# First feed-forward network's weights: product and low half moved from GpSimd to VectorE, two layer norms moved with them, one ScalarE wait later, and other lengths in the planner's list

## The chip, the cores and the metric

The kernel runs on one core of one Trainium2 chip. The metric is device time in microseconds (us), as the median of several executions. The engines are named TensorE (PE), VectorE (DVE), ScalarE (ACT), GpSimd (POOL) and SyncE (SP) in the text and by the short names in the profile.

## What is computed

Two transformer layers on x of shape (4, 512, 512), each with two sublayers and a layer norm after each sum:

```python
x = layernorm(x + L0_attn(x))    # causal attention, 32 query heads, 8 key heads, head size 16, rotary
x = layernorm(x + L0_ffn(x))     # 512 -> 1376 -> 512, SiLU gate; weights packed as 4-bit numbers
x = layernorm(x + L1_attn(x))    # a "hydra" state-space mixer, two passes
x = layernorm(x + L1_ffn(x))     # 512 -> 1792 -> 512, SiLU gate; weights as int32 with scale and zero
```

The weights of the first feed-forward network (FFN) are `w = q*s - (z+1)*s`, where q is one of eight 4-bit numbers in an int32, s a float16 scale and z a 4-bit zero. Those of the second are `(w - z)*s`.

## The kernel before

**Tiling.** The 2048 tokens are 16 tiles of 128. Attention runs in 352 units; a unit is a group of heads of one query tile (scores in PSUM, `nmax`, `exp`, transposes `ptr`, a high half `pth` and a low half `ptl` in float16, then `pv`). Matrices are held as a float16 high half and a float16 low half, so each product of an FFN takes three matmuls.

**Order of the work.** The class `Stream` (from line 169) is a planner that runs on the host while the kernel is built. It lists every step with its engine, an assumed length in ns, what it waits for and a rank. `place()` (line 407) runs the list by events: each engine takes, of its ready steps, the one with the lowest rank. The result is one fixed order for each engine, and each engine executes its own order strictly, waiting on semaphores where the real lengths differ from the assumed ones. So a wait of one step holds back everything listed behind it on that engine. The assumed lengths are no instructions: they only decide the order. For SP a step holds the engine for `SP_ISSUE` (1300 ns for all kinds) and ends after its listed length. `START_AT` says when each engine's stream begins.

**First FFN's weights.** They come in 27 chunks (`CH0`, line 146): 16 of 128x688 for gate and up, 11 of 128x512 for down (the last of 96 rows). Chunk c has rank 2c-2, so the planner ties two attention units to each chunk. A chunk runs: three loads by SP (`sp_w0`, lines 702 to 711: packed numbers to `pk`, zeros to `zb`, scales to the low half's place); VectorE takes the 4 bits out (L1166) and forms q minus z (L1169); GpSimd multiplies by the scale (`pool_dequant`, L839, to `wv`); ScalarE rounds the high half (L1043); GpSimd subtracts to get the low half (`pool_dequant_lo`, L846). `wv`, `pk`, `zb` and `nib` have two buffers. The first gate and up matmul of the first FFN (L1538) waits for the low half of the last chunk (`w0_lo`, NC0), since all of w0 must be there.

**Second FFN's weights.** 84 chunks of 128x256, after the last chunk of the first: three loads by SP (L720 to L722), three operations on GpSimd (L851, L853, L855: `w1_q`), the high half on ScalarE (L1048, which also waits for the stores of the chunk before), the low half on GpSimd (L859), two stores to DRAM (L727, L728). Two buffers. They are loaded back as whole matrices only when the first FFN is done with its gate and up matmuls.

**Norms.** `bn1` and `bn2` gather mean and variance on VectorE (L1133 to L1136); GpSimd forms 1/sqrt (L872) and normalises (L874), for all 16 tiles and both norms of the first layer. The norms of the second layer form 1/sqrt on GpSimd and normalise on VectorE (L1381, L1408).

**Start.** VectorE unpacks the zeros of the first FFN (L1438, L1442), SP stores them to DRAM (L817). ScalarE issues six small loads, then waits for all three stores, then starts its stream with the copy `xT` of the first tile (L979), for which the first projections (L1498) wait. The buffers of the zeros lie where `xh`, `xl`, `attn`, `aT` and `wo` are used later; VectorE and GpSimd have waits of their own on the stores.

Of the kernel before, what the change touches and what calls it, by code (L numbers as in the profile page):

```python
# [79 lines left out]
RING = 8  # L80
# [92 lines left out]
class Stream:  # L173
# [46 lines left out]
    def weights0(self):  # L220
        A = self.add
        for c, (k, g, c0, n) in enumerate(CH0):
            r = CH0_AT[c]
            A("SP", "w0", c, 3000, [("deq", c - 2)] if c >= 2 else [], r - 6)
            A("DVE", "deq", c, 1500 if n == HW else 1200, [("w0", c)], r)
            A("POOL", "deq_w", c, 1600 if n == HW else 1230, [("deq", c), ("w0_lo", c - 2) if c >= 2 else None], r)
            A("ACT", "w0_hi", c, 780 if n == HW else 600, [("deq_w", c)], r)
            A("POOL", "w0_lo", c, 1600 if n == HW else 1230, [("w0_hi", c)], r)

    def weights1(self):  # L230
        A = self.add
        for c in range(NC1):
            r = CH1_AT[c]
            A("SP", "w1c", c, 3000, [("w1_lo", c - 2) if c >= 2 else ("w0_lo", NC0 - 1)], r - 6)
            A("POOL", "w1_q", c, 1950, [("w1c", c)], r)
            A("ACT", "w1_hi", c, 420, [("w1_q", c), ("w1s", c - 1) if c else None], r)
            A("POOL", "w1_lo", c, 720, [("w1_hi", c)], r)
            A("SP", "w1s", c, 2500, [("w1_lo", c)], r)
# [22 lines left out]
    def attention(self, u):  # L261
        A = self.add
        t, i, w, h, g = UNITS[u]
        c = w * g
        need = [("e" + kind, t) for kind in STAGE]
        A("PE", "score", u, 0.42 * c + 55 * g, need + [("exp", u - 2) if u >= 2 else None], u)
        A("DVE", "nmax", u, 150 + 1.07 * c, [("score", u), ("exp", u - 4) if u >= 4 else None], u - 1)
        A("ACT", "exp", u, 200 * g + 0.75 * c, [("nmax", u), ("ptr", u - 2) if u >= 2 else None], u - 1)
        A("PE", "ptr", u, 110 * c // P, [("exp", u), ("ptl", u - 2) if u >= 2 else None], u + 2.1)
        A("ACT", "pth", u, 170 + 0.84 * c, [("ptr", u), ("pv", u - 3) if u >= 3 else None], u)  # L270
        A("DVE", "ptl", u, 150 + 1.07 * c, [("pth", u)], u)
        q = group_of(u)
        new = h % OG == 0
        A("PE", "pv", u, 52 * (i + 1) * g, [("ptl", u), ("out", q - 1) if new and q else None], u + 4.2)
        if ends_group(u):
            A("DVE", "out", q, 620, [("pv", u), ("attn", q - 2) if q >= 2 else None], u)
            A("POOL", "attn", q, 500, [("out", q), ("atr", t - 2) if q % NOG == 0 and t >= 2 else None], u)

    def way_out(self, t):
        A, r = self.add, END[t] + 5  # L280
        A("PE", "atr", t, 440, [("attn", NOG * t + NOG - 1)], r, takes=1)
        A("ACT", "ate", t, 610, [("atr", t), ("wo", t - 1, WO_PIECES - 1) if t else None], r, frees=("atr", t))
        e = self.pieces("wo", t, WO_PIECES, 860, [("ate", t)], r)
        A("DVE", "x1_sum", t, 690, [e], r, frees=("wo", t))
        A("DVE", "bn1", t, 1100, [("x1_sum", t), ("x1", t - 2) if t >= 2 else None], r)
        A("POOL", "x1", t, 1500, [("bn1", t)], r - 4)

    def ffn0(self, h):
# [17 lines left out]
        for x in (0, 1):  # L306
# [6 lines left out]
            A("POOL", "x2_sum", t, 1400, [("y16", t), ("x1", t)], soon - 4)  # L313
            A("DVE", "bn2", t, 1100, [("x2_sum", t), ("x2", t - 2) if t >= 2 else None], soon)
            A("POOL", "x2", t, 1500, [("bn2", t)], soon - 4)
# [100 lines left out]
    def place(self):  # L416
# [40 lines left out]
        while done < len(self.steps):  # L457
# [17 lines left out]
            at[e] = t + (SP_ISSUE if e == "SP" else ns + GAP)  # L475
# [22 lines left out]
SLACK, GAP, SP_ISSUE = 150, 0, 1300  # L498
START_AT = {"PE": 5100, "ACT": 6400, "DVE": 12600, "POOL": 5100, "SP": 15000}
# [10 lines left out]
def build(nc, A):  # L510
# [12 lines left out]
    with ctx:  # L523
# [308 lines left out]
        def pool_dequant(pool, c):  # L832
            k, g, c0, n = CH0[c]
            r = rows0(k, g)
            hi, lo = (w0[k][p][0:r, g, c0:c0 + n] for p in (0, 1))
            pool.wait_ge(sem("deq_z"), c + 1)
            if c >= 2:
                pool.wait_ge(sem("w0_lo"), c - 1)
            pool.tensor_tensor(wv[0:r, c % 2, 0:n], hi, lo, ALU.mult).then_inc(sem("deq_w"), 1)  # L839

        def pool_dequant_lo(pool, c):
            k, g, c0, n = CH0[c]
            r = rows0(k, g)
            hi, lo = (w0[k][p][0:r, g, c0:c0 + n] for p in (0, 1))
            pool.wait_ge(sem("w0_hi"), c + 1)
            pool.tensor_tensor(lo, wv[0:r, c % 2, 0:n], hi, ALU.subtract).then_inc(sem("w0_lo"), 1)  # L846

# [13 lines left out]
        def pool_job(pool, kind, key):  # L861
# [5 lines left out]
            if kind in ("x1", "x2"):  # L867
                n, v, r, m = ("1", ve, rstd, mv) if kind == "x1" else ("2", veb, rstdb, mvb)
                o = key % 2
                x = xr[:, key % RING, :]  # L870
                pool.wait_ge(sem(f"ve{n}"), key + 1)
                pool.tensor_tensor(r[:, o:o + 1], v[:, o:o + 1], neghalf[:, 0:1], ALU.pow).then_inc(sem(f"rstd{n}"), 1)  # L872
                pool.wait_ge(sem(f"rstd{n}"), key + 1)
                pool.tensor_scalar(x, x, m[:, o, 0:1], r[:, o:o + 1], ALU.subtract, ALU.mult).then_inc(sem(kind), 1)  # L874
# [31 lines left out]
        def pool_stream(pool):  # L906
            for name in STREAM.order["POOL"]:
                kind, key = name[0], name[1]
                if kind in ("x1", "x2", "x2_sum", "attn", "f0_lo", "qk", "q_lo", "k_lo"):
                    pool_job(pool, kind, key)  # L910
                if kind == "deq_w":
                    pool_dequant(pool, key)
                if kind == "w0_lo":
                    pool_dequant_lo(pool, key)
# [108 lines left out]
        def act_attention(act, kind, u):  # L1023
# [6 lines left out]
            if kind == "exp":  # L1030
                act.wait_ge(sem("nmax"), u + 1)
# [86 lines left out]
        def _(act):  # L1118
# [7 lines left out]
            for k in "gud":  # L1126
                act.wait_ge(sem(f"st_zs_{k}"), 16)
# [34 lines left out]
        def dve_dequant(dve, c):  # L1162
# [7 lines left out]
                                     in1=zb[0:r, c % 2, 0:n], op0=ALU.mult, op1=ALU.subtract).then_inc(sem("deq_z"), 1)  # L1170

# [14 lines left out]
        def dve_job(dve, own, kind, key):  # L1186
# [41 lines left out]
            if kind == "bn1":  # L1228
                dve.wait_ge(sem("x1_sum"), t + 1)
                if t >= 2:  # L1230
                    dve.wait_ge(sem("x1"), t - 1)
                layer_norm_1(dve, own, x, st6, mv[:, o, :], ve[:, o:o + 1], sem("ve1"))
            if kind == "fxl":
# [4 lines left out]
            if kind == "bn2":  # L1238
                dve.wait_ge(sem("x2_sum"), t + 1)
                if t >= 2:  # L1240
                    dve.wait_ge(sem("x2"), t - 1)
                layer_norm_1(dve, own, x, st6b, mvb[:, o, :], veb[:, o:o + 1], sem("ve2"))
# [167 lines left out]
        def dve_stream(dve, own):  # L1410
            for name in STREAM.order["DVE"]:
# [3 lines left out]
                if kind in ("qk_c", "qk_s", "v", "etq1", "etk1", "x1_sum", "bn1", "fxl", "bn2"):  # L1415
# [3 lines left out]
                if kind == "deq":  # L1419
                    dve_dequant(dve, key)  # L1420
                if kind in ("consts_a", "consts_b", "consts_c"):
# [365 lines left out]
```

## Time and profile before

| | |
|---|---|
| median of 3 runs | 1624.26 us (1624.23 to 1624.38) |
| profiled execution's own time | 1626.21 us |
| its span | 1624.0 us |
| PE busy | 1454.7 us (90%) |
| DVE busy | 1081.7 us (67%) |
| ACT busy | 802.8 us (49%) |
| POOL busy | 773.4 us (48%) |
| mean granted TensorE clock | 0.957 of full |

The span is the profiled execution from its first to its last instruction. The busy share of an engine is a mean over stages with different limits; the stages are the first 184 us (first attention units beside the unpacking of the first FFN's weights), then up to about 880 us attention beside the first FFN and the second FFN's weights, then the hydra stages and the second FFN.

### The profile page before, as it was taken

To read this page: it belongs to the slowest core of one execution; us is meant where nothing else is said; L and a number is where in the kernel's file an instruction comes from. 1 tells how busy PE (TensorE), PEld (TensorE's weight loads), DVE (VectorE), ACT (ScalarE), POOL (GpSimd) and SP (SyncE) were. 2 spreads that over 40 slices of the span, in tenths; PEclk is the share of its full clock that TensorE was granted. 3 is DMA by queue.
4 is the path that set the end of the run, shared out by engine and by line. 5 is a ranking of instruction groups with operands and counts; after the bars stand their busy time and mean duration, and the time that the engine had idled before them with its cause. 6 is when DMAs were issued, how large, how long until landed. Compare 5 with 4: busy or idle time off the path is not lost.

```text
span 1624.0 us, 33859 instructions
## 1 busy us (share of the span) xinstructions
PE 1454.7 (90%) x12464; PEld 1081.9 (67%) x12464; DVE 1081.7 (67%) x2353; ACT 802.8 (49%) x1723; POOL 773.4 (48%) x918
## 2 busy tenths in 40 slices
PE   4767899978899889999999989569999999999998
PEld 2555676766676678686886857337666776857865
DVE  4898776755666667675877876757779679772121
ACT  2566666755656667675766843223333433412211
POOL 3776666566566666666222136424343343332211
PEclk9878799999999999999999999869999999999999
DMA  5433233233433232332002000450100000100000
GB/s 188 128 104 95 67 80 91 67 75 94 105 79 81 68 92 62 104 88 88 9 2 72 28 30 14 175 187 2 34 7 14 27 14 1 40 7 8 14 14 14
DMA packets 94221, 100.34 MB, mean 62 GB/s; under 512 B 11565, under 2 KB 76672, under 8 KB 94056
## 3 DMA queue, kind: packets, MB, share of 16 engines
q1 hardware_dynamic: 92818, 98.10, 21.2%
q8 instruction: 100, 1.64, 0.4%
q14 instruction: 65, 0.53, 0.1%
q10 hardware_dynamic: 1238, 0.07, 0.1%
HBM read 78.70 MB, written 19.43 MB: 60 GB/s over the span
## 4 chain that ended last, share of the span: by engine, by line
PE 40%; DVE 22%; POOL 13%; DMA 11%; issue 6%; SPq 5%; ACT 3%; DVEq 0%; ACTq 0%; POOLq 0%
PE ps L1703 10%; PE ps L1538 5%; PE ps L1601 4%; DMA vs<-in_s1g 4%; DMA vs<-in_s1u 3%; PE ps L1723 3%; PE ps L1553 3%; PE ps L1525 2%; PE ps L1591 2%; DVE xraw L1324 2%; DMA vs<-in_s1d 2%; POOL xr L874 2%; POOL vl L859 2%; PE ps L1651 2%; POOL vq L851 2%
## 5 line engine op out<-in xcount | busy, mean ns | idle before, releaser
L1159 DVE TENSOR_REDUCE nmax<-ps 128x1 f32<-128x384 f32 (+3 forms) x352 | 218.9, 634 | 83.1 <-PE ps L1594 79.9
L1035 ACT ACTIVATE Pe<-ps,nmax 128x256 f32<-128x256 f32 (+3 forms) x512 | 247.0, 535 | 31.3 <-DVE nmax L1159 30.2
L1029 ACT ACTIVATE pth<-ps 128x512 f16<-128x512 f32 (+1 forms) x352 | 196.7, 561 | 130.7 <-PE ps L1601 127.2
L1154 DVE TENSOR_TENSOR ptl<-ps,pth 128x512 f16<-128x512 f32 (+1 forms) x352 | 217.4, 632 | 32.9 <-ACT pth L1029 30.8
L1601 PE MATMUL ps<-identf,Pe 128*128 128x128 f32 x1280 | 208.8, 283 | 10.2 <-DVE ptl L1154 10.0
L1591 PE MATMUL ps<-kT,qT 128*128 128x256 f16 (+3 forms) x512 | 142.2, 311 | 35.1 <-ACT Pe L1035 34.5
L1601 PEld LDWEIGHTS ps<-identf,Pe 128*128 128x128 f32 x1280 | 144.6, 147 | 42.0 <-issue 20.8
L941 POOL TENSOR_TENSOR int1l<-prod,int1h 128x256 f16<-128x256 f32 x112 | 86.4, 776 | 175.6 <-ACT int1h L1115 175.6
L1703 PE MATMUL ps<-x3h,w1gh 128*128 128x256 f16 x448 | 123.3, 275 | 4.9 <-DVE prod L1394 3.8
L1703 PE MATMUL ps<-x3h,w1uh 128*128 128x256 f16 x448 | 123.4, 275 | 0.0
L1703 PE MATMUL ps<-x3l,w1gh 128*128 128x256 f16 x448 | 123.4, 275 | 0.0
L1703 PE MATMUL ps<-x3h,w1gl 128*128 128x256 f16 x448 | 123.3, 275 | 0.0
L1703 PE MATMUL ps<-x3l,w1uh 128*128 128x256 f16 x448 | 123.3, 275 | 0.0
L1703 PE MATMUL ps<-x3h,w1ul 128*128 128x256 f16 x448 | 123.2, 275 | 0.0
L851 POOL TENSOR_TENSOR vq<-vq,vz 128x256 int32<-128x256 int32 x84 | 61.1, 727 | 115.4 <-DMA vs<-in_s1g 47.2
L1109 ACT ACTIVATE sg<-ps 128x256 f32<-128x256 f32 x112 | 42.2, 380 | 147.1 <-PE ps L1703 146.6
L1394 DVE SCALAR_TENSOR_TENSOR prod<-ps,sg 128x256 f32<-128x256 f32 x112 | 46.9, 424 | 99.5 <-ACT sg L1109 94.6
L1614 PE MATMUL ps<-V,pth 128*128 128x34 f16 x1280 | 92.5, 180 | 17.0 <-DVE ptl L1154 15.7
L1614 PEld LDWEIGHTS ps<-V,pth 128*128 128x128 f16 x1280 | 86.6, 98 | 30.2 <-DVE ptl L1154 20.2
L866 POOL TENSOR_TENSOR int0l<-prod,int0h 128x256 f16<-128x256 f32 (+1 forms) x88 | 60.4, 687 | 90.1 <-ACT int0h L1016 89.9
L1594 PE MATMUL ps<-mask,identb 128*128 128x128 bf16 x512 | 102.4, 226 | 0.0
L1115 ACT ACTIVATE int1h<-prod 128x256 f16<-128x256 f32 x112 | 46.0, 417 | 109.2 <-DVE prod L1394 109.2
(236 smaller groups left out, 4067.1 us busy)
## 6 DMA issues: line engine op xcount, KB each, us to landing
xr<-in_x SPq DMA_DIRECT2D x16, 256.0 KB, 4.8
x_dram<-xr SPq DMA_DIRECT2D x16, 256.0 KB, 2.0
x2a<-x_dram SPq DMA_DIRECT2D x4, 1024.0 KB, 4.8
x<-x_dram SPq DMA_DIRECT2D x4, 1024.0 KB, 5.1
out<-x SPq DMA_DIRECT2D x16, 256.0 KB, 2.0
vq<-in_q1g SPq DMA_DIRECT2D x28, 128.0 KB, 2.2
vz<-in_z1g SPq DMA_DIRECT2D x28, 128.0 KB, 3.9
vs<-in_s1g SPq DMA_DIRECT2D x28, 128.0 KB, 4.5
```

The costliest lines, as they stand in the source:

```text
L851: pool.tensor_tensor(q.bitcast(I32), q.bitcast(I32), vz[:, c % 2, :], ALU.subtract).then_inc(sem("w1_i"), 1)
L941: pool.tensor_tensor(int1[1][:, j, :], prod1[:, key % 2, :], int1[0][:, j, :], ALU.subtract).then_inc(sem("f1_lo"), 1)
L1029: act.activation(pth[:, u % 3, 0:g * w], ps[:, 2 + u % 2, 0:g * w], ACT.Copy).then_inc(sem("pth"), 1)
L1035: ins = act.activation(Pe[:, u % 2, x * w:(x + 1) * w], ps[:, u % 2, x * w:(x + 1) * w], ACT.Exp, bias=nmax[:, u % 4, x:x + 1])
L1154: dve.tensor_tensor(ptl[:, u % 3, 0:g * w], ps[:, 2 + u % 2, 0:g * w], pth[:, u % 3, 0:g * w], ALU.subtract).then_inc(sem("ptl"), 1)
L1159: dve.tensor_reduce(nmax[:, u % 4, 0:g], ps[:, u % 2, 0:g * w].rearrange("p (g w) -> p g w", g=g), AX, ALU.max, negate=True).then_inc(sem( ...
L1538: ins = pe.matmul(ps[0:r, bank, cols], w0[m][pw][:, k, c0:c0 + r], px[:, k, :], start=(k == 0 and at == 0), stop=(k == KD - 1 and at == 2))
L1591: pe.matmul(ps[:, u % 2, x * w:(x + 1) * w], qT[:, h // 2, i * P:(i + 1) * P], kT[:, 2 * (h // NREP) + h % 2, first:first + w], start=True ...
L1594: ins = pe.matmul(ps[:, u % 2, at:at + P], identb[:, :], mask[:, :], start=False, stop=True)
L1601: ins = pe.transpose(ps[:, 2 + u % 2, c:c + P], Pe[:, u % 2, c:c + P], identf[:, :])
L1614: ins = pe.matmul(dst, src[:, u % 3, c:c + P], V[:, b % 2, token_tile(b, i, p), h // NREP, :], start=(part == 0 and p == 0), stop=(part == ...
L1703: ins = pe.matmul(ps[:, bank, piece * H2:piece * H2 + H2], w1[m][pw][:, k, j * P:(j + 1) * P], px[:, k, h * H2:h * H2 + H2], start=(at == ...
```

## The change

1. **Unpacking.** L839 and L846 leave GpSimd; the same two `tensor_tensor` operations stand on VectorE as `dve_product` and `dve_low_half`, with the same waits. A chunk is then VectorE four times and ScalarE once.
2. **ScalarE's wait** for the three stores of the zeros moves from ahead of its stream to ahead of the first `exp`.
3. **Norms 1 and 2.** GpSimd keeps 1/sqrt (`rstd1`, `rstd2`), VectorE normalises (`x1`, `x2`). The waits of `bn1` and `bn2` on the norm two tiles earlier go, as both are now in VectorE's own order.
4. **The planner's lengths.** Loads of the first FFN's chunks 6500 instead of 3000 ns, of the second's 5700 instead of 3000, its stores 3600 instead of 2500, `attn` 430 instead of 500, `x2_sum` 1200 instead of 1400; SP held 850 to 4500 ns by kind instead of 1300; VectorE's stream starts at 13100 instead of 12600, SP's at 17500 instead of 15000.

```diff
-            A("SP", "w0", c, 3000, [("deq", c - 2)] if c >= 2 else [], r - 6)
-            A("DVE", "deq", c, 1500 if n == HW else 1200, [("w0", c)], r)
-            A("POOL", "deq_w", c, 1600 if n == HW else 1230, [("deq", c), ("w0_lo", c - 2) if c >= 2 else None], r)
+            A("SP", "w0", c, 6500, [("deq", c - 2)] if c >= 2 else [], r - 6)
+            A("DVE", "deq", c, 1500 if n == HW else 1150, [("w0", c)], r)
+            A("DVE", "deq_w", c, 900 if n == HW else 690, [("deq", c), ("w0_lo", c - 2) if c >= 2 else None], r)
             A("ACT", "w0_hi", c, 780 if n == HW else 600, [("deq_w", c)], r)
-            A("POOL", "w0_lo", c, 1600 if n == HW else 1230, [("w0_hi", c)], r)
+            A("DVE", "w0_lo", c, 900 if n == HW else 690, [("w0_hi", c)], r)
...
-            A("SP", "w1c", c, 3000, [("w1_lo", c - 2) if c >= 2 else ("w0_lo", NC0 - 1)], r - 6)
+            A("SP", "w1c", c, 5700, [("w1_lo", c - 2) if c >= 2 else ("w0_lo", NC0 - 1)], r - 6)
...
-            A("SP", "w1s", c, 2500, [("w1_lo", c)], r)
+            A("SP", "w1s", c, 3600, [("w1_lo", c)], r)
...
-            A("POOL", "attn", q, 500, [("out", q), ("atr", t - 2) if q % NOG == 0 and t >= 2 else None], u)
+            A("POOL", "attn", q, 430, [("out", q), ("atr", t - 2) if q % NOG == 0 and t >= 2 else None], u)
...
-        A("POOL", "x1", t, 1500, [("bn1", t)], r - 4)
+        A("POOL", "rstd1", t, 600, [("bn1", t)], r - 4)
+        A("DVE", "x1", t, 570, [("rstd1", t)], r - 4)
...
-            A("POOL", "x2_sum", t, 1400, [("y16", t), ("x1", t)], soon - 4)
+            A("POOL", "x2_sum", t, 1200, [("y16", t), ("x1", t)], soon - 4)
             A("DVE", "bn2", t, 1100, [("x2_sum", t), ("x2", t - 2) if t >= 2 else None], soon)
-            A("POOL", "x2", t, 1500, [("bn2", t)], soon - 4)
+            A("POOL", "rstd2", t, 600, [("bn2", t)], soon - 4)
+            A("DVE", "x2", t, 570, [("rstd2", t)], soon)
...
-            at[e] = t + (SP_ISSUE if e == "SP" else ns + GAP)
+            at[e] = t + (SP_ISSUE.get(name[0], 450) if e == "SP" else ns + GAP)
...
-SLACK, GAP, SP_ISSUE = 150, 0, 1300
-START_AT = {"PE": 5100, "ACT": 6400, "DVE": 12600, "POOL": 5100, "SP": 15000}
+SLACK, GAP = 150, 0
+SP_ISSUE = {"w0": 1900, "w1c": 1300, "w1s": 850, "weights_a": 4500, "weights_b": 1700, "w1_load": 1300}
+START_AT = {"PE": 5100, "ACT": 6400, "DVE": 13100, "POOL": 5100, "SP": 17500}
...
-            if kind in ("x1", "x2"):
-                n, v, r, m = ("1", ve, rstd, mv) if kind == "x1" else ("2", veb, rstdb, mvb)
+            if kind in ("rstd1", "rstd2"):
+                v, r = (ve, rstd) if kind == "rstd1" else (veb, rstdb)
                 o = key % 2
-                x = xr[:, key % RING, :]
-                pool.wait_ge(sem(f"ve{n}"), key + 1)
-                pool.tensor_tensor(r[:, o:o + 1], v[:, o:o + 1], neghalf[:, 0:1], ALU.pow).then_inc(sem(f"rstd{n}"), 1)
-                pool.wait_ge(sem(f"rstd{n}"), key + 1)
-                pool.tensor_scalar(x, x, m[:, o, 0:1], r[:, o:o + 1], ALU.subtract, ALU.mult).then_inc(sem(kind), 1)
+                pool.wait_ge(sem("ve1" if kind == "rstd1" else "ve2"), key + 1)
+                pool.tensor_tensor(r[:, o:o + 1], v[:, o:o + 1], neghalf[:, 0:1], ALU.pow).then_inc(sem(kind), 1)
...
             if kind == "exp":
+                if u == 0:
+                    for k in "gud":
+                        act.wait_ge(sem(f"st_zs_{k}"), 16)
                 act.wait_ge(sem("nmax"), u + 1)
...
             act.wait_ge(sem("consts"), 1)
-            for k in "gud":
-                act.wait_ge(sem(f"st_zs_{k}"), 16)
             act_stream(act)
...
+        def dve_product(dve, c):
+            k, g, c0, n = CH0[c]
+            r = rows0(k, g)
+            hi, lo = (w0[k][p][0:r, g, c0:c0 + n] for p in (0, 1))
+            dve.wait_ge(sem("deq_z"), c + 1)
+            if c >= 2:
+                dve.wait_ge(sem("w0_lo"), c - 1)
+            dve.tensor_tensor(wv[0:r, c % 2, 0:n], hi, lo, ALU.mult).then_inc(sem("deq_w"), 1)
+
+        def dve_low_half(dve, c):
+            k, g, c0, n = CH0[c]
+            r = rows0(k, g)
+            hi, lo = (w0[k][p][0:r, g, c0:c0 + n] for p in (0, 1))
+            dve.wait_ge(sem("w0_hi"), c + 1)
+            dve.tensor_tensor(lo, wv[0:r, c % 2, 0:n], hi, ALU.subtract).then_inc(sem("w0_lo"), 1)
...
             if kind == "bn1":
                 dve.wait_ge(sem("x1_sum"), t + 1)
-                if t >= 2:
-                    dve.wait_ge(sem("x1"), t - 1)
                 layer_norm_1(dve, own, x, st6, mv[:, o, :], ve[:, o:o + 1], sem("ve1"))
+            if kind in ("x1", "x2"):
+                m, r = (mv, rstd) if kind == "x1" else (mvb, rstdb)
+                dve.wait_ge(sem("rstd1" if kind == "x1" else "rstd2"), t + 1)
+                dve.tensor_scalar(x, x, m[:, o, 0:1], r[:, o:o + 1], ALU.subtract, ALU.mult).then_inc(sem(kind), 1)
```

## Rows read from the trace of the kernel before

**Rows 1.** Stretches: busy PE, PEld, DVE, ACT, POOL (instructions), clock, DMA share, GB/s.

```profile
0.00:40.00 40.00, 19.06 (x76) 11.59 (x76) 16.60 (x45) 8.38 (x12) 15.40 (x26) 0.95 0.61 191
40.00:184.00 144.00, 104.13 (x908) 76.20 (x909) 128.78 (x204) 90.45 (x191) 100.34 (x80) 0.80 0.36 99
184.00:880.00 696.00, 649.78 (x6484) 499.13 (x6483) 462.42 (x944) 444.07 (x981) 406.30 (x569) 0.99 0.29 74
880.00:1100.00 220.00, 179.01 (x1391) 130.13 (x1389) 159.95 (x379) 99.77 (x186) 81.12 (x67) 0.88 0.24 85
```

**Rows 2.** What TensorE waited for, 184 to 880 us: total us, times, longest.

```profile
PE ps L1591 <- ACT Pe L1035: 22.3, 20, 3.1
PE ps L1484 <- POOL attn L888: 8.2, 6, 2.4
```

**Rows 3.** The same of ScalarE.

```profile
ACT vh L1048 <- POOL vq L855: 47.8, 22, 4.8
ACT vh L1048 <- DMA w_ul<-vl: 18.0, 8, 4.6
```

**Rows 4.** The same of GpSimd.

```profile
POOL vq L851 <- DMA vs<-in_s1g: 47.2, 21, 4.4
...
POOL vq L851 <- DMA vs<-in_s1d: 25.5, 19, 2.5
```

**Rows 5.** Timeline to 30 us: start, length, engine, operation, idle before and releaser.

```profile
1.17 0.42 SPq L811 DMA_DIRECT2D wqkv<-in_wqkvT  x1
...
14.58 1.28 ACT L979 ACT_TABLE_LOAD   x1 [14.58 <-DMA zs_d<-zs]
...
16.62 6.68 PE L1498 MATMUL ps<-wqkv,xT 128*128 128x512 f32 x8 [10.40 <-ACT xT L979]
...
25.16 0.82 DVE L1202 TENSOR_TENSOR qk_c<-ps,costab 128x640 f32<-128x640 f32 x1 [12.07 <-PE ps L1501]
...
29.60 0.57 DVE L1166 TENSOR_SCALAR nib<-pk,shift 128x688 int32<-128x688 int32 x1
```

**Rows 6.** DMA issues: count, size, median us from issue to landing.

```profile
vs<-in_s1g SPq DMA_DIRECT2D x28, 128.0 KB, 4.5
wqkv<-in_wqkvT SPq DMA_DIRECT2D x1, 1536.0 KB, 7.0
```

**Rows 7.** Operations by line: ns min/median/max, first and last start us, forms.

```profile
L1166 DVE TENSOR_SCALAR nib<-pk,shift x27: 473/982/1886, 27.2 to 178.9; 128x688 int32<-128x688 int32 x16, 128x512 int32<-128x512 int32 x10, 96x512 int32<-96x512 int32 x1
L1169 DVE SCALAR_TENSOR_TENSOR w0dh<-nib,zb x11: 689/693/2497, 123.6 to 179.4; 128x512 f16<-128x512 int32 x10, 96x512 f16<-96x512 int32 x1
L1169 DVE SCALAR_TENSOR_TENSOR w0uh<-nib,zb x8: 876/1635/2686, 46.8 to 117.8; 128x688 f16<-128x688 int32 x8
L1538 PE MATMUL ps<-xh,w0gh x352: 269/272/421, 185.6 to 1019.0; 128*128 128x256 f16 x160, 128*96 128x256 f16 x16
L859 POOL TENSOR_TENSOR vl<-vq,vh x84: 667/672/681, 194.0 to 759.8; 128x256 f16<-128x256 f32 x84
```

**Rows 8.** Busy time of L1166, L1169, L839, L846 in turn, 40 to 184 us.

```profile
40.00:184.00 144.00, 23.96 (x24) 0.80 0.36 99
...
40.00:184.00 144.00, 30.91 (x25) 0.80 0.36 99
...
40.00:184.00 144.00, 36.51 (x25) 0.80 0.36 99
...
40.00:184.00 144.00, 38.32 (x27) 0.80 0.36 99
```

**Rows 9.** The norm on GpSimd, and its like on VectorE: ns min/median/max.

```profile
L874 POOL TENSOR_SCALAR xr<-xr,mvb,rstdb x16: 2080/2082/2876, 271.1 to 1049.9; 128x512 f32<-128x512 f32 x16
L1381 DVE TENSOR_SCALAR x<-x,mvc,rstdc x16: 536/545/548, 1079.6 to 1465.2; 128x512 f32<-128x512 f32 x16
```

**Rows 10.** Chain that ended last, 860 to 1230 us: start, us, what.

```profile
991.48 2.08 POOL xr L874
...
1049.94 2.08 POOL xr L874
```

More of the change, by code:

```diff
@@ L829, in dn_bank @@
             return BC_BANK if s else JOB_BANK["c1_dn", (0, 0)]
[L832 to L846, printed above, removed]
         def pool_w1(pool, c):
@@ L908, in pool_stream @@
                 kind, key = name[0], name[1]
-                if kind in ("x1", "x2", "x2_sum", "attn", "f0_lo", "qk", "q_lo", "k_lo"):
+                if kind in ("rstd1", "rstd2", "x2_sum", "attn", "f0_lo", "qk", "q_lo", "k_lo"):
                     pool_job(pool, kind, key)
[L911 to L914, printed above, removed]
                 if kind == "w1_q":
@@ L1239, in dve_job @@
                 dve.wait_ge(sem("x2_sum"), t + 1)
-                if t >= 2:
-                    dve.wait_ge(sem("x2"), t - 1)
                 layer_norm_1(dve, own, x, st6b, mvb[:, o, :], veb[:, o:o + 1], sem("ve2"))
@@ L1414, in dve_stream @@
                     dve_gate(dve, kind, key)
-                if kind in ("qk_c", "qk_s", "v", "etq1", "etk1", "x1_sum", "bn1", "fxl", "bn2"):
+                if kind in ("qk_c", "qk_s", "v", "etq1", "etk1", "x1_sum", "bn1", "x1", "fxl", "bn2", "x2"):
                     dve_job(dve, own, kind, key)
@@ L1420, in dve_stream @@
                     dve_dequant(dve, key)
+                if kind == "deq_w":
+                    dve_product(dve, key)
+                if kind == "w0_lo":
+                    dve_low_half(dve, key)
                 if kind in ("consts_a", "consts_b", "consts_c"):
```

## The prediction

> **What bounds the kernel now.** I read the busy time by stretches first, then the waits of each engine inside the stretches, then single operations. Three stages matter here [rows 1]. From 40 to 184 us TensorE is busy 104.1 of 144 us at a granted clock of 0.80 of full, that is partly at its lower level of 1.2 GHz, while VectorE is busy 128.8 and GpSimd 100.3: VectorE is the bound, with 15.2 us idle, and GpSimd is close behind. From 184 to 880 us TensorE is busy 649.8 of 696 us at clock 0.99, so its matmuls are the bound and all that can be won is its 46.2 us of idle time. From 880 to 1100 us TensorE leaves 41 us idle beside chains of small steps; the reader should look there for GpSimd steps on the chain. Behind 1100 us nothing is touched but by a shift of what went before.
>
> Who causes the 46.2 us is the second reading. TensorE waited 22.3 us for ScalarE's `exp` and 8.2 us for `attn` on GpSimd [rows 2]. Each engine runs a fixed order, so I ask what ScalarE stood at. It waited 47.8 us for the second FFN's chunks to come from GpSimd and 18.0 us for the stores of one matrix [rows 3]; two more such rows for the other two matrices are of the same kind. And GpSimd waited for the loads of these chunks: 47.2 and 25.5 us are the largest and the smallest of three rows, one for each matrix [rows 4]. A load lands 4.5 us after its issue [rows 6], and it is the last of three issues, where the planner lists 3.0 for all three. So the chunk steps stand too early in the orders of GpSimd and ScalarE, and attention queues behind them.
>
> **Part A, the later ScalarE wait.** TensorE has been idle for 10.40 us, since 6.2, when the projections start at 16.62; ScalarE, which copies the first tile for them, starts at 14.58, behind the store of the zeros [rows 5]. Without the wait they need the copy and the weights: those are issued at 1.17 + 0.42 [rows 5] and land 7.0 later [rows 6], at 8.6. That is 8.0 us earlier, and VectorE's first step on them moves from 25.16 to about 17. What is late next is VectorE's own stream, which still waits for the stores, to 14.5 (ScalarE's start shows when they had landed), so it is ahead of 17. I take -7 us, with ends of -8 and 0 (0 if the packed weights' loads, whose issue times don't move, pace VectorE then). The moved wait ahead of `exp` costs nothing: the stores landed by 14.5 and no `exp` can run before the first scores.
>
> **Part B, 54 operations from GpSimd to VectorE.** The trace has no such operation on VectorE; nearest is L1169, also with two SBUF inputs, 876 ns for 688 elements and 689 for 512 when undisturbed [rows 7]. So 32 x 0.876 + 22 x 0.689 = 28.0 + 15.2 = 43.2 us of new VectorE work before 184 us. Against it stands a relief. L1166 and L1169 take 23.96 + 30.91 = 54.9 us from 40 to 184 [rows 8]. Undisturbed, their 24 and 25 operations would take 13 x 0.57 + 11 x 0.473 = 12.6 and 14 x 0.876 + 11 x 0.689 = 19.8 us [rows 5, 7], so 22.5 us are stretch; one of 0.876 took 2.69 [rows 7]. I put it down to GpSimd working beside them, 100.3 us of 144 [rows 1], of which L839 and L846 are 36.5 + 38.3 = 74.8 [rows 8]. The rest is 25.5, and 21.3 without the two norms of 2.08 that fall there [rows 9]: a fifth of before. So 4.8 us of the old stretch stay, and the new operations get as much in proportion, 22.5/32.4 x 43.2 x 0.21 = 6.3. VectorE's sum is 43.2 - 22.5 + 4.8 + 6.3 + 1.1 (two norms of 0.545, [rows 9]) = +33 us.
>
> How much of that lengthens the stage? VectorE has 15.2 us idle there; I let it absorb two thirds, 10. So +23 us, and with part A the first matmul of the first FFN, which waits for the last low half and now starts at 185.6 [rows 7], comes about 16 later, near 202. Bounds: no stretch left and all idle time absorbed gives 33 - 11 - 15 = +7; nothing absorbed and half of the old stretch staying gives 43.2 - 11 + 1 = +33. I take +23. It counts in full, since until then TensorE has attention alone and no filler; after it TensorE is full. ScalarE's part (L1043) is unchanged.
>
> The trace shows the stretch: operations of the same shape at 0.876 and 2.69 us while GpSimd is busy. The Trainium skill, "SBUF — State Buffer", section "Who interferes with whom", has the rule behind it, and it speaks against this part: VectorE and GpSimd share one port pair as an exclusive lock, and a VectorE instruction with two SBUF inputs takes part in it. By that rule both new operations can be held up as the old ones were, whereas a VectorE of its own ports would give +43 - 22 = +21 without a term for new stretch; the stretch term of 6.3 is small here only because so little GpSimd work is left.
>
> **Part C, the lists.** With 5.7 us for a chunk's loads the planner puts the GpSimd and ScalarE steps of the 84 chunks later, behind attention steps that are ready. Of TensorE's idle time 22.3 + 8.2 = 30.5 us hang on those two engines [rows 2]. I take two thirds, -20 us; the ends are 0 (waits only move) and -35 (three quarters of all 46.2). Also some 23 of the 32 norms leave GpSimd in this stretch, 2.08 us each; on VectorE they cost 23 x 0.545 = 13 us, hidden by its 696 - 462 = 234 us idle [rows 1, 9]. If the cover is gone they cost those 13. The norm adds a wait: VectorE now waits for 1/sqrt from GpSimd, with `nmax` and `ptl` queued behind it and ScalarE and TensorE behind those. If GpSimd stands at a load just then, up to 4.4 us are lost, with 25.5/19 to 47.2/21, 1.3 to 2.2 us, usual [rows 4]; at 23 norms that is at most 51 us of VectorE time against 234 idle. I take it as nothing and keep it for the rival. If the second FFN's weights are ready later (the last low half now stands at 759.8), nobody waits before the first FFN has ended its gate and up, at 1019 [rows 7]. SP's other issues keep their order but for the longer listing; their instructions are the same.
>
> **Part D, the last norms.** On the chain that ended last GpSimd's norm stands three times between 991 and 1052 us (the first and the last in [rows 10], the one between at its longest, 2.88 [rows 9]), 7.0 us in all, ahead of hydra steps on GpSimd. On VectorE they are 3 x 0.545 = 1.6, on an engine that is itself on that chain. At most -5.4; I take -4, with an upper end of +2 (VectorE queues them in front of hydra steps).
>
> **The sum.** -7 + 23 - 20 - 4 = -8 us. The profiled execution took 1626.2 us, so 1618.2 by its measure; the median of the runs is 1.95 lower: about 1616 us.
>
> **Rivals.**
> 1. *VectorE becomes the bound and its waits spread* (slower). Mechanism: the first stage grows by its upper end, +33, and VectorE waiting for 1/sqrt gives the in-order waits back, so that C yields 8 instead of 20; D yields 2. -7 + 33 - 8 - 2 = +16: 1640 us. For it: VectorE is already at 89% there. Against: GpSimd's load falls by three quarters. It decides when the first FFN's start moves by more than C and D give back: with 24 us given back, beyond 210 us.
> 2. *Each GpSimd operation left holds VectorE for its whole length* (no change). Nearly every VectorE operation of the unpacking then meets one: all of the 21.3 us left on GpSimd are added in place of 4.8 + 6.3. That is +10 on my sum: 1626 us. For it: one operation of 0.876 us took 2.69 [rows 7], longer by more than a whole GpSimd operation of the unpacking (74.8/52 = 1.44 us, [rows 8]). Against: the stretch of 22.5 us is only a quarter of GpSimd's 100.3 [rows 1]. This is what the exclusive lock of the Trainium skill's page quoted above would do if every pair met.
> 3. *Gain and loss cancel* (no change). Stage +16 with A, C gives 14, D 4: 1622 us. For it: the new order still rests on listed lengths that differ from real ones, such as 1.5 us for L1166 and L1169 together, whose medians are 982 and 1635 ns [rows 7].
> 4. *The start and the lists win fully.* Stage +7 - 8, C -30, D -5: -36, 1588 us. For it: the relief is measured and VectorE has idle time. Against: three quarters of a saturated engine's idle time have never gone by a reordering of one kind of step.
> 5. *It doesn't do what it says*: the new order differs so that part A is lost, as when VectorE's first step stands behind a load landing at about 25 us. Then +7 on my sum: 1623 us.
>
> **How the numbers follow.** Forecast 0.46 (1606 to 1621 as its own range); rival 1 0.22; rival 2 0.06; rivals 3 and 5 0.12 together; rival 4 0.14. A difference of 0.2%, 3.2 us, is about what a measurement can tell from none. Faster than 1621.0: nearly all of the forecast (0.42) and rival 4 (0.14), and a little of rival 3 (0.02): 0.58. Slower than 1627.5: rival 1 (0.22) and the upper parts of rivals 2, 3 and 5 (0.06) make 0.28. Within: 0.14. For the range of 8 in 10 I cut half of rival 4 at the low end and a third of rival 1 at the high end: 1592 to 1640.
>
> **What would show it.** Part A: first projections near 8.6 us, `qk_c` near 17. Part B: the new operations at 0.88 and 0.69 us with little above, L1166 and L1169 near 36 us in sum, first FFN matmul near 202 us. Part C: ScalarE's waits at L1048 and GpSimd's at L851 down by half or more, TensorE's idle time from there to 880 us down to some 26 us. Part D: no norm of GpSimd on the chain. I am wrong if the first FFN matmul comes well before 192 (the first stage was paced by GpSimd, not VectorE), or if the waits for loads fall while TensorE's idle time doesn't.

## The result

The changed kernel takes 1594.6 us against 1624.2 us before, ratio 0.983 (95% interval 0.981 to 0.985): 29.6 us faster, where the text above forecast 8. The time is near the low end of the stated range, so the sign was right and the size was not. The profiled execution took 1594.41 us, its span is 1592.6.

The same stretches as [rows 1], of the changed kernel; the columns are the same:

```profile
0.00:40.00 40.00, 27.10 (x136) 16.41 (x136) 20.05 (x51) 11.95 (x19) 15.81 (x26) 0.96 0.57 183
40.00:184.00 144.00, 93.34 (x752) 66.00 (x751) 126.15 (x215) 77.30 (x160) 20.17 (x22) 0.74 0.33 91
184.00:880.00 696.00, 677.08 (x6883) 528.07 (x6883) 519.25 (x1055) 478.34 (x1043) 363.56 (x551) 0.99 0.29 80
880.00:1100.00 220.00, 173.76 (x1315) 129.35 (x1316) 165.92 (x406) 87.83 (x176) 74.73 (x68) 0.89 0.21 76
```

From 40 to 184 us TensorE does less (93.3 us against 104.1, clock 0.74 against 0.80) and GpSimd stands nearly empty. From 184 to 880 us TensorE is idle for 18.9 us where it was 46.2. The waits behind that, from 184 to 880 us, as in [rows 2 to 4]:

```profile
PE ps L1592 <- ACT Pe L1018: 6.6, 9, 1.4
```

```profile
ACT vh L1031 <- POOL vq L842: 1.1, 2, 0.6
...
POOL vq L838 <- DMA vs<-in_s1u: 20.7, 11, 5.3
...
POOL vq L838 <- DMA vs<-in_s1d: 3.2, 3, 1.4
...
POOL vq L838 <- DMA vs<-in_s1g: 1.4, 2, 1.1
```

Each row gives total us, times, longest. TensorE's wait for `exp` is down from 22.3 to 6.6 us, ScalarE's for chunks from 47.8 to 1.1, GpSimd's for the loads of the last matrix from 25.5 to 3.2 and of the first from 47.2 to 1.4. The start, as in [rows 5], and the new operations in the first 220 us:

```profile
8.33 5.95 PE L1499 MATMUL ps<-wqkv,xT 128*128 128x512 f32 x8 [2.12 <-ACT xT L959]
...
16.14 0.82 DVE L1199 TENSOR_TENSOR qk_c<-ps,costab 128x640 f32<-128x640 f32 x1 [2.97 <-PE ps L1502]
```

```profile
L1147 DVE TENSOR_SCALAR nib<-pk,shift 128x688 int32<-128x688 int32 (+2 forms) x27 | 16.2, 602 | 0.0
L1150 DVE SCALAR_TENSOR_TENSOR w0gh<-nib,zb 128x688 f16<-128x688 int32 x8 | 9.2, 1145 | 0.3
L1150 DVE SCALAR_TENSOR_TENSOR w0dh<-nib,zb 128x512 f16<-128x512 int32 (+1 forms) x11 | 8.3, 755 | 0.4
L1167 DVE TENSOR_TENSOR w0gl<-wv,w0gh 128x688 f16<-128x688 f32 x8 | 8.2, 1020 | 0.0
L1167 DVE TENSOR_TENSOR w0dl<-wv,w0dh 128x512 f16<-128x512 f32 (+1 forms) x11 | 7.7, 700 | 0.1
L1160 DVE TENSOR_TENSOR wv<-w0dh,w0dl 128x512 f32<-128x512 f16 (+1 forms) x11 | 7.5, 686 | 0.2
L1160 DVE TENSOR_TENSOR wv<-w0gh,w0gl 128x688 f32<-128x688 f16 x8 | 7.3, 916 | 0.2
L1150 DVE SCALAR_TENSOR_TENSOR w0uh<-nib,zb 128x688 f16<-128x688 int32 x8 | 7.0, 876 | 0.3
L1160 DVE TENSOR_TENSOR wv<-w0uh,w0ul 128x688 f32<-128x688 f16 x8 | 7.0, 871 | 0.2
L1167 DVE TENSOR_TENSOR w0ul<-wv,w0uh 128x688 f16<-128x688 f32 x8 | 6.9, 866 | 0.0
```

The columns are busy us, mean ns of one, idle before. L1147 and L1150 are L1166 and L1169 of the kernel before, L1160 is the product and L1167 the low half. The old pair of operations takes 16.2 + 24.5 = 40.7 us for 27 chunks and the new pair 44.6.

**Three parts and a ledger.** The kernels below are best compared between two marks in each trace: TensorE's first and last gate and up matmul of the first FFN. Ahead of the first mark lies the first stage, between them attention beside the first FFN, behind them the rest. Before, then changed; columns: stretch, length, TensorE busy (instructions), clock, DMA share, GB/s.

```profile
0.00:185.60 185.60, 124.79 (x992) 0.83 0.41 119
185.60:1019.00 833.40, 777.58 (x7642) 0.99 0.26 67
1019.00:1624.00 605.00, 552.30 (x3835) 0.95 0.10 37
```

```profile
0.00:213.20 213.20, 142.37 (x1054) 0.78 0.36 103
213.20:983.50 770.30, 752.62 (x7556) 0.99 0.27 72
983.50:1592.60 609.10, 550.34 (x3863) 0.96 0.10 37
```

The first stage is 27.6 us longer, the middle 63.1 us shorter, the rest 4.1 us longer: -31.4 us in the spans. TensorE's idle time goes from 60.8 to 70.8 us in the first, from 55.8 to 17.7 in the middle and from 52.7 to 58.8 in the rest. So the change holds a loss and a gain that is twice as large, and the question is which edit makes which. Such rows come from one execution each. In the kernel before and in four kernels below that change only the lengths of the second FFN's chunks, every engine runs the same order up to the first mark, and that stage still took 181.0 to 185.6 us; so differences of up to 5 us in one stage are not read as effects.

### The profile page after: what moved, and what is told of

Same layout as the page of the kernel before. It is cut to its first block, busy times and chain, and to the rows that moved or that the text cites. A ratio compares the mean times of both kernels' runs of the same rounds, so it can differ in the third digit from the quotient of the medians.

```text
span 1592.6 us, 33841 instructions
## 1 busy us (share of the span) xinstructions
PE 1445.3 (91%) x12464; PEld 1080.8 (68%) x12464; DVE 1120.3 (70%) x2439; ACT 804.9 (51%) x1723; POOL 629.8 (40%) x832
## 4 chain that ended last, share of the span: by engine, by line
PE 67%; DVE 23%; issue 5%; ACT 3%; POOL 1%; DMA 0%; DVEq 0%; SPq 0%; POOLq 0%; ACTq 0%
PE ps L1539 14%; PE ps L1704 10%; PE ps L1602 9%; PE ps L1554 6%; PE ps L1592 5%; PE ps L1499 4%; PE ps L1526 4%; PE ps L1615 3%; PE ps L1724 3%; DVE xraw L1321 3%; PE ps L1502 2%; PE ps L1485 2%; PE ps L1595 2%; PE ps L1652 2%; PE ps L1517 1%
## 5 line engine op out<-in xcount | busy, mean ns | idle before, releaser
L1602 PE MATMUL ps<-identf,Pe 128*128 128x128 f32 x1280 | 212.3, 287 | 1.8 <-DVE ptl L1135 1.7
L1602 PEld LDWEIGHTS ps<-identf,Pe 128*128 128x128 f32 x1280 | 147.2, 149 | 31.4 <-issue 9.2
L1704 PE MATMUL ps<-x3h,w1uh 128*128 128x256 f16 x448 | 122.5, 273 | 0.0
L1615 PE MATMUL ps<-V,pth 128*128 128x34 f16 x1280 | 91.7, 179 | 18.9 <-DVE ptl L1135 13.7
L1539 PE MATMUL ps<-xh,w0gh 128*128 128x256 f16 (+1 forms) x352 | 96.4, 274 | 7.5 <-DVE xl L1235 6.1
```

Of the source, the lines that this page charges most:

```text
L1539: ins = pe.matmul(ps[0:r, bank, cols], w0[m][pw][:, k, c0:c0 + r], px[:, k, :], start=(k == 0 and at == 0), stop=(k == KD - 1 and at == 2))
L1602: ins = pe.transpose(ps[:, 2 + u % 2, c:c + P], Pe[:, u % 2, c:c + P], identf[:, :])
L1615: ins = pe.matmul(dst, src[:, u % 3, c:c + P], V[:, b % 2, token_tile(b, i, p), h // NREP, :], start=(part == 0 and p == 0), stop=(part == ...
L1704: ins = pe.matmul(ps[:, bank, piece * H2:piece * H2 + H2], w1[m][pw][:, k, j * P:(j + 1) * P], px[:, k, h * H2:h * H2 + H2], start=(at == ...
```

## Experiments: each part alone

All ratios are to runs of the kernel before on the same chip; its medians there were 1626.2, 1624.1 and 1625.2 us in the order of the three groups below. The groups ran on different chips, so between groups the ratios are compared.

**The later ScalarE wait alone.**

```diff
             if kind == "exp":
+                if u == 0:
+                    for k in "gud":
+                        act.wait_ge(sem(f"st_zs_{k}"), 16)
                 act.wait_ge(sem("nmax"), u + 1)
...
             act.wait_ge(sem("consts"), 1)
-            for k in "gud":
-                act.wait_ge(sem(f"st_zs_{k}"), 16)
             act_stream(act)
```

> The kernel before with one edit: ScalarE's wait for the stores of the zeros stands ahead of the first exp. The orders of all engines are those of before. If the prediction's part A holds (the start pays in full, since VectorE bounds the first stage): -7 us, first projections at 8.3 us as in the changed kernel. Rival (GpSimd and the chunk loads pace the first stage, or later in-order waits take the time back): 0 to -2 us.

Measured: 1623.0 us, 0.997 (0.996 to 0.999), some 4 us. The first FFN matmul comes at 176.1 us, 9.5 earlier than before, but the middle grows from 833.4 to 840.0 us:

```profile
0.00:176.10 176.10, 120.84 (x992) 0.85 0.44 125
176.10:1016.10 840.00, 781.33 (x7641) 0.98 0.27 66
1016.10:1621.20 605.10, 552.43 (x3835) 0.95 0.10 37
```

The earlier start reaches the first mark in full. Most of it is lost again in the middle: 2.9 us there are more idle time of TensorE, the other 3.8 more busy time for the same instructions, at clock 0.98 instead of 0.99. GpSimd's waits for the loads are those of before (116.1 us for 115.2). Why the middle grew was not tried by itself.

**Two listed lengths alone.** No instruction differs from before, only the orders.

```diff
-            A("SP", "w1c", c, 3000, [("w1_lo", c - 2) if c >= 2 else ("w0_lo", NC0 - 1)], r - 6)
+            A("SP", "w1c", c, 5700, [("w1_lo", c - 2) if c >= 2 else ("w0_lo", NC0 - 1)], r - 6)
...
-            A("SP", "w1s", c, 2500, [("w1_lo", c)], r)
+            A("SP", "w1s", c, 3600, [("w1_lo", c)], r)
```

> The kernel before with only two listed lengths changed: loads of the second FFN's chunks 5700 instead of 3000 ns, its stores 3600 instead of 2500. No instruction changes, only the orders. Theory L (the lists make most of the gain): TensorE's idle time between the first matmul of the first FFN (185.6 us before) and 880 us falls from 46 to about 20 us and the time by 20 us or more. Theory R (GpSimd's relief makes it: with some 144 us of work less on GpSimd its in-order waits vanish by themselves): at most -8 us.

Measured: 1577.5 us, 0.970 (0.967 to 0.973): 48.7 us faster than before and faster than the changed kernel. By the marks:

```profile
0.00:181.00 181.00, 123.00 (x991) 0.84 0.43 122
181.00:970.60 789.60, 766.25 (x7642) 0.99 0.28 70
970.60:1575.30 604.70, 551.84 (x3835) 0.96 0.11 37
```

The rest is unchanged, and the middle holds 43.8 of the 48.7 us: idle time from 55.8 to 23.4, and 11.3 us less busy time for the same 7642 instructions. The first stage's 4.6 us are within the spread named above. Theory L holds, with more than it expected.

**The unpacking's move alone**, L839 and L846 to VectorE (`dve_product`, `dve_low_half`) with their listed lengths:

```diff
-            A("POOL", "deq_w", c, 1600 if n == HW else 1230, [("deq", c), ("w0_lo", c - 2) if c >= 2 else None], r)
+            A("DVE", "deq_w", c, 900 if n == HW else 690, [("deq", c), ("w0_lo", c - 2) if c >= 2 else None], r)
...
-            A("POOL", "w0_lo", c, 1600 if n == HW else 1230, [("w0_hi", c)], r)
+            A("DVE", "w0_lo", c, 900 if n == HW else 690, [("w0_hi", c)], r)
```

> The kernel before with only the product and the low half of the first FFN's chunks moved to VectorE (listed 900 or 690 ns). Theory L: slower, as the first stage grows by 20 to 28 us and the waits for the second FFN's loads stay: +10 to +20 us. Theory R: the first stage grows, but the later stages pay it back: -5 us or better. VectorE's sum of the two old operations near 41 us instead of 61 under both.

Measured: 1631.2 us, 1.0035 (1.0016 to 1.0053): slower, but by 6 us only, so both theories miss the size.

```profile
0.00:207.60 207.60, 128.17 (x982) 0.79 0.37 106
207.60:1023.40 815.80, 773.62 (x7650) 0.99 0.27 68
1023.40:1628.20 604.80, 552.04 (x3835) 0.95 0.11 37
```

The first stage grows by 22.0 us as theory L has it, and the middle gives 17.6 back, 13.6 of them idle time. In this order GpSimd waits less for the chunk loads, 81.0 us in the whole trace instead of 115.2. Why that order has fewer such waits was not followed up. The last group below shows that the repayment is gone once those waits are: there the middle takes 785.3 us with the move and 782.7 without.

**The norms' move alone**, instructions and list:

```diff
-        A("POOL", "x1", t, 1500, [("bn1", t)], r - 4)
+        A("POOL", "rstd1", t, 600, [("bn1", t)], r - 4)
+        A("DVE", "x1", t, 570, [("rstd1", t)], r - 4)
...
-            A("POOL", "x2", t, 1500, [("bn2", t)], soon - 4)
+            A("POOL", "rstd2", t, 600, [("bn2", t)], soon - 4)
+            A("DVE", "x2", t, 570, [("rstd2", t)], soon)
```

> The kernel before with only the two norms of the first layer moved to VectorE. Prediction's part D: -4 us, from the chain behind 990 us. Theory R: more, -8 to -12 us, since 32 x 2.08 = 67 us leave GpSimd's order. Theory L: -4 or less.

Measured: 1612.2 us, 0.991 (0.989 to 0.994), 14 us faster, more than either theory had.

```profile
0.00:181.30 181.30, 124.09 (x992) 0.83 0.43 122
181.30:1000.90 819.60, 769.11 (x7618) 1.00 0.28 68
1000.90:1609.40 608.50, 553.83 (x3859) 0.95 0.10 37
```

Most of it lies in the middle (-13.8); the first stage's -4.3 is within the spread named above. Of the middle's 13.8 us, 5.3 are idle time and 8.5 busy time, with 24 instructions fewer. It isn't that GpSimd waits less for the chunk loads: those waits rise from 115.2 to 131.1 us. TensorE's wait for `exp` in the middle falls from 22.8 to 18.1. What makes the gain stays open.

Behind the last mark, where the prediction looked for it, the kernel is 3.5 us longer, but those 24 instructions now stand there. A fairer mark is the last `pv` matmul, before and then with the norms alone (the second time is the start of the last one):

```profile
L1614 PE MATMUL ps<-V,ptl x1280: 177/177/193, 54.9 to 939.4; 128*128 128x34 f16 x183
```

```profile
L1613 PE MATMUL ps<-V,ptl x1280: 177/177/193, 52.0 to 926.9; 128*128 128x34 f16 x183
```

So 12.5 us lie ahead of it. Behind it the kernel before takes 684.6 us and this one 682.5, with 18 gate and up matmuls fewer, which one every 0.11 us make 2.0 us. A gain of 4 us there is not to be seen.

## Experiments: undoing parts of the change

**The two lengths back in the changed kernel** (5700 to 3000 and 3600 to 2500, the reverse of the diff above).

> The changed kernel with the two lengths of the second FFN's chunks as before (loads 3000, stores 2500 ns). Theory L (those lengths carry the gain, whatever else is changed): slower than before, 1594.6 + 30 to 45 us = 1625 to 1640 us, with ScalarE's and GpSimd's waits for the chunks back at 80 us or more. Rival N (any new order is 10 to 50 us better by chance, as the one before was an unlucky one): stays near 1595 us.

Measured: 1645.0 us, 1.013 (1.011 to 1.014) of before: the changed kernel without them is slower than the kernel before, by more than theory L expected. They carry 49 us in it by the ratios (50.4 by the medians). GpSimd's waits for the chunk loads are back, larger than before:

```profile
POOL vq L838 <- DMA vs<-in_s1g: 59.3, 22, 16.8
POOL vq L838 <- DMA vs<-in_s1u: 53.3, 24, 5.1
...
POOL vq L838 <- DMA vs<-in_s1d: 31.3, 18, 3.1
```

Rival N, a lucky order, falls: the same two numbers are worth 48.7 us in one setting and 49 in another.

**The unpacking back on GpSimd in the changed kernel** (the reverse of the diff above).

> The changed kernel with product and low half back on GpSimd, with their lengths of before. Theory U (moving them to VectorE is a loss that the lengths hide): faster than the changed kernel by 8 to 20 us, that is 1575 to 1587 us, with the first matmul of the first FFN earlier than 213 us. Rival V (with good lengths the relief of GpSimd is worth having): slower than the changed kernel.

Measured: 1569.7 us, 0.966 (0.965 to 0.968): 24.9 us faster than the changed kernel by the medians, 26 by the ratios. Theory U holds in the time and fails in its mark:

```profile
0.00:218.90 218.90, 167.37 (x1459) 0.91 0.36 104
218.90:954.60 735.70, 714.91 (x7147) 1.00 0.31 75
954.60:1568.00 613.40, 555.03 (x3863) 0.95 0.10 37
```

The first FFN matmul comes still later, at 218.9 us; the list of this kernel has the first FFN's loads at 6500 instead of 3000 ns, which is the likely reason and was not tried by itself. But the planner runs attention meanwhile, 1459 TensorE instructions instead of 1054, at clock 0.91 with 51.5 us idle. The place of that matmul is no measure of loss; TensorE's idle time and its clock are.

**The kernel before with three of the changes**: the wait, the norms and the two lengths.

> The kernel before with the later ScalarE wait, the norms on VectorE and the two longer lengths of the second FFN's chunks, but the first FFN's unpacking and all other lengths as before. Theory U with parts that add: 1626 x 0.970 = 1577, less 4 for the wait (0.9973) and up to 14 for the norms (0.9914): 1560 to 1573 us, faster than both kernels. If the norms' gain came from the same in-order waits as the lengths' gain, it is mostly used up: 1570 to 1577 us. Rival N: anything between 1560 and 1620 us.

Measured: 1571.3 us, 0.968 (0.966 to 0.969). It equals the last one within their spread, and both beat the kernel before by 53 to 54 us and the changed kernel by 23 to 26. The norms and the wait together add 4 to 6 us to the lengths alone, where they had 14 and 4 singly. So their gains overlap with that of the lengths; by which waits isn't shown, since the norms alone left GpSimd's waits for the loads longer.

**The loads' length alone** (5700 instead of 3000, the stores' at 2500).

> The kernel before with only the listed length of the second FFN's loads at 5700 ns; stores stay at 2500. Theory L with the loads as the cause: most of the 49 us of the two lengths together (30 us or more); GpSimd's waits for loads fall from 115 to about 20 us, while ScalarE still waits some 40 us for stores. If the stores matter as much: half, 20 to 30 us.

Measured: 1575.5 us, 0.971 (0.969 to 0.974). The loads are the cause; the stores' length adds nothing that can be measured. GpSimd's remaining waits for the loads:

```profile
POOL vq L851 <- DMA vs<-in_s1u: 25.2, 13, 5.9
...
POOL vq L851 <- DMA vs<-in_s1g: 8.6, 9, 1.9
...
POOL vq L851 <- DMA vs<-in_s1d: 4.0, 3, 2.0
```

## Experiments: sizes

**Loads listed at 4300 and at 8000 ns**, in the kernel before, one number changed.

> The kernel before with the second FFN's loads listed at 4300 ns, halfway from 3000 to 5700. Theory L (a listed length below the real one of about 6 us puts the waits in front of attention): between the two, 1590 to 1610 us, with some 60 us of GpSimd's waits for loads left. Rival N (any other order is better): near 1576 us.

> The kernel before with the second FFN's loads listed at 8000 ns, above the real length. Theory L: the waits for loads stay away (below 38 us at L851) and nothing more is gained: 1570 to 1582 us, as long as the chunks still end well before the first FFN does. Rival N: anything. Should the chunks end later than the first FFN's last gate and up matmul (about 970 us), their loading back is late and the time goes up.

| listed, ns | ratio to before | interval | middle, us | GpSimd's waits for the loads, us |
|---|---|---|---|---|
| 3000 (before) | 1 | | 833.4 | 115.2 |
| 4300 | 0.978 | 0.975 to 0.981 | 802.9 | 70.9 |
| 5700 | 0.971 | 0.969 to 0.974 | 788.5 | 37.8 |
| 8000 | 0.972 | 0.969 to 0.975 | 791.9 | 0 |

The real length, from the issue of a chunk's first load to the landing of its third, is 5.3 us in the median of the 84 chunks of the kernel before (3.9 to 7.1). The gain follows the waits up to about that length. Beyond it the last 37.8 us of waits go too and nothing more comes. Theory L expected 1590 to 1610 us for 4300 and 1570 to 1582 for 8000; the medians are 1588.5 and 1579.8, and rival N's 1576 for 4300 falls. 8000 costs nothing that can be measured against 5700, 4300 costs 12 us and 3000 costs 47.

**The move again, under good lengths**: both operations, and the low half alone, on top of the kernel with three of the changes.

> The kernel without the unpacking's move (1571.3 us) with that one edit added: product and low half on VectorE. Theory U (24.4 us of added VectorE work before the first FFN's first matmul count about in full, once the chunk loads are listed well): 1571 + 15 to 25 = 1586 to 1596 us, TensorE's idle time in the first 184 us up from 55 to some 70 us. Rival V (it costs only with the other changed lengths): within 5 us of 1571.

> As the kernel without the unpacking's move, but with the low half alone on VectorE, 27 operations, the product staying on GpSimd. Theory U with costs that follow VectorE's work: half of the added 43 us of operations, and half of the stretch relieved: about +8 to +12 us on 1571, that is 1579 to 1583. If VectorE has a step in it (absorbs some, then nothing): below 1575.

Measured: 1599.8 us (0.985, 0.981 to 0.988) with both, 1586.2 (0.976, 0.973 to 0.979) with the low half alone, against 1571.3. That is +28.5 and +14.9 us by the medians, +27 and +13 by the ratios: half for half in time, and both above what was expected. The first stage without the move, with both, by engine as in [rows 1]:

```profile
0.00:177.40 177.40, 122.53 (x992) 86.49 (x993) 147.13 (x252) 100.03 (x203) 112.53 (x104) 0.85 0.43 125
```

```profile
0.00:204.20 204.20, 131.56 (x982) 90.46 (x983) 165.92 (x300) 100.18 (x200) 37.48 (x49) 0.73 0.38 107
```

With the low half alone:

```profile
0.00:191.70 191.70, 132.05 (x992) 90.35 (x993) 153.04 (x277) 100.58 (x203) 75.24 (x76) 0.75 0.41 114
```

With both, VectorE has 18.8 us more work and the stage is 26.8 us longer. With the low half alone VectorE has only 5.9 us more, and the stage is 14.3 us longer. So in both cases some 8 us come on top of VectorE's own work, in which VectorE is idle. Seen from TensorE, 17.8 of the 26.8 us are idle time, 54.9 to 72.6, and 9.0 busy time, with ten instructions fewer; of the 14.3 us, 4.8 are idle and 9.5 busy, with the same 992 instructions. The granted clock fell from 0.85 to 0.73 and 0.75, which is the likely source of most of the added busy time. A stretch of TensorE near 101 us in the kernel with the move:

```profile
100.85 0.42 PE L1591 MATMUL ps<-kT,qT 128*128 128x256 f16 x1
101.07 0.31 PE L1594 MATMUL ps<-mask,identb 128*128 128x128 bf16 x1
101.17 1.06 PE L1601 MATMUL ps<-identf,Pe 128*128 128x128 f32 x4
```

and without it:

```profile
100.39 0.27 PE L1591 MATMUL ps<-kT,qT 128*128 128x256 f16 x1
100.50 0.22 PE L1594 MATMUL ps<-mask,identb 128*128 128x128 bf16 x1
100.55 0.61 PE L1601 MATMUL ps<-identf,Pe 128*128 128x128 f32 x4
```

The same shapes take 0.42 and 1.06 us at 1.2 GHz and 0.27 and 0.61 at 2.4. By the trace's record of the clock the lower level held for 53.9 us of the stage without the move, 97.0 with the low half and 108.4 with both. TensorE's idle stretches became more, not longer: 53, 63 and 69 in the stage, about 1 us each in the mean. Most of the added ones are waits for `exp`, 11.5 us in total without the move, 19.3 with the low half, 25.6 with both. With both, `exp` itself waited longer for VectorE's `nmax` (26.2 us for 9.9), with the low half alone it did not (10.4). So how the move breaks up TensorE's work isn't fully shown.

**The path from one kernel to the other**, by the ratios to the kernel before: two lengths -49 us, wait and norms -4, the move +27, the other lengths -3. The sum is about -28. The last step can't be told from nothing, since the two ratios that it rests on are 0.981 to 0.988 and 0.981 to 0.985.

## Why the prediction was right or wrong

**Part A** took -7 us. The start came as worked out: projections at 8.33 where 8.6 was said, `qk_c` at 16.14 for 17. In the time it was 4 us alone, since the middle took 6.6 back; the assumption that an earlier first stage counts in full failed.

**Part B** took +23 us and measured +25 to +26 when undone in the changed kernel and +27 to +28.5 under good lengths; alone it was +6. The terms: new operations 43.2 said, 44.6 measured; L1166 and L1169 [rows 7] fall from 60.9 us in the whole trace to 40.7; VectorE's net is +24.4, and +25.5 with two norms, where +33 was said: the new operations were stretched by 1.4 us and not by 6.3, and the old ones gave back 20.2 us and not 17.7. So the time came near by luck: the work was put 7.5 us too high, and the 10 us of it that VectorE's idle time was to absorb were not absorbed. The stage grew by 8 us more than VectorE's work in it, with VectorE idle for them and TensorE at a lower clock, which the sum left out. "It counts in full" held where the loads were listed well; with the old list the middle gave 17.6 us back. Rival 2, with every GpSimd operation holding VectorE, falls: it added all of GpSimd's 21.3 us, and the stretch of old and new operations together is 4.8 + 1.4 us. With GpSimd busy 20.2 us instead of 100.3 from 40 to 184 us, L1166 and L1169 are 5 us over their undisturbed 35.9 (16 x 0.57 + 11 x 0.473 + 16 x 0.876 + 11 x 0.689) instead of 25. That is the direction of the rule of the Trainium skill, "SBUF — State Buffer", section "Who interferes with whom", that a VectorE instruction with two SBUF inputs contends with a GpSimd instruction that reads SBUF.

**Part C** took -20 us and is the step that failed. Its mechanism was right and the term mis-sized: the lengths are worth some 49 us, and even its end of -35 was too small. Its ceiling was TensorE's idle time from 184 to 880 us, of which I took two thirds of the 30.5 us that hang on ScalarE and GpSimd. The runs show two things left out. The middle runs to 1019 us and has 55.8 us idle, of which 32.4 went. And the busy time fell by 11.3 us with the same instructions. The second is the lesson, and it has two sources, which give an estimate of 11.3 together and were not tried singly. A matmul is shown 0.27 us long while the next one starts 0.11 us after it (L1591 and L1594 in the last rows above), so an interruption leaves some 0.16 us of tail that counts as busy; TensorE's idle stretches in the middle fell from 72 to 37, which makes 5.6 us. And of its busy time in the middle 19.3 us stood at 1.2 GHz before and 8.0 after, which at half the speed makes 5.7 us.

**Part D** took -4 us from the chain behind 990 us. No norm stands on GpSimd's part of the chain after the change, as said, and still no gain shows there: behind the last `pv` matmul the kernel with the norms alone is 2.1 us shorter, for 18 matmuls fewer. The norms gained their 14 us nearly all ahead of it, where the text had booked them at nothing, and most of that is gone once the lengths are right.

**The sum.** By the ratios, part C gave -49 for -20, parts A and D together -4 for -11, part B +27 for +23, and the other lengths, which had no term, -3. The miss is part C's, and the others partly hid it.

**Rivals.** The outcome is nearest to rival 4 in time (1588) but not in its make: its stage of -1 was really +27 or so, and its -30 for the lists was too small. Rival 1 was right that VectorE becomes the bound of the first stage, and the changed kernel without the two lengths ends at 1645 us, near its 1640. **The mark** was badly chosen: the first FFN matmul came at 213 us, later than the 210 from which the change should have lost.

## What to carry to other kernels

Where each engine runs a fixed order, compare every assumed length with the trace first, transfers above all: one number that was little more than half the real one (3.0 us for 5.3) cost 3% here, and correcting it alone beats the whole change. When a wait holds up an engine that isn't the bound, don't cap its price by the idle time of the bound; undo it and see. And measure the parts of a bundle singly: this one hid a loss of 25 to 28 us behind a gain of 49. A stage's length from a single trace moved by up to 5 us here with nothing changed in it.

## What the runs showed of the hardware

TensorE's granted clock was lower where its work was broken up more often, with idle stretches of about the same mean length: 992 instructions of the first stage took 122.5 us at 0.85 with 53 idle stretches and 132.1 us at 0.75 with 63. A `tensor_tensor` with two SBUF inputs on VectorE took 866 to 871 ns for 688 elements in the least disturbed groups (the most disturbed one 1020) and 686 to 700 for 512, whether both inputs were float16 or one of them float32.
